# Values of a cross attention made for four pairs of heads at once, in 512 columns, and weights and x turned first

## The reference, cut to what matters

```
r = sigmoid(x @ Wr.T); k = x @ Wk.T; v = x @ Wv.T       # weights are made ternary first
state = cumsum(k*v / scale) * scale                      # over tokens
x = layernorm(x + rmsnorm(r*state, ln_w) @ Wo.T)
q = x @ Wq + bq; k = ctx @ Wk + bk; v = ctx @ Wv + bv    # 16 heads of 64
x = layernorm(x + softmax(q k.T / 8) v @ Wo + bo)
x = layernorm(x + moe(x))     # top 1 of 8 experts, capacity 512, 128 -> 512 -> 128
```

## Time and profile before

| | us |
|---|---|
| median of 3 runs | 2730.99 (2728.54 to 2731.56) |
| profiled execution | 2729.38 |
| its span, first to last instruction | 2727.6 |
| TensorE busy | 2659.0 |
| VectorE busy | 2122.0 |
| GpSimd busy | 2152.3 |
| ScalarE busy | 1723.4 |
| mean granted clock of TensorE | 0.989 of 2.4 GHz |

### The profile page before, as it was taken

One profiled execution on the slowest core, in us unless ns is written; L12 is line 12 of the kernel. 1 busy time (PEld: TensorE's weight loads), 2 busy tenths in 40 slices (PEclk: granted clock), 3 DMA queues, 4 the chain that ended last, 5 costly groups with the idle time before them and its releaser, 6 DMA issues.

```text
span 2727.6 us, 67860 instructions
## 1 busy us (share of the span) xinstructions
PE 2659.0 (97%) x26920; PEld 2280.4 (84%) x26920; DVE 2122.0 (78%) x4293; ACT 1723.4 (63%) x3470; POOL 2152.3 (79%) x1749
## 2 busy tenths in 40 slices
PE   5999999999999999999999999999999999999977
PEld 5888888888888888888888888888888888888855
DVE  6687878788787887878778787878878788787744
ACT  3666676666666666756657666666666666666632
POOL 1778888888788877888878888888888787888845
PEclk7999999999999999999999999999999999999988
DMA  4000000000000000000000000000000000000030
GB/s 101 7 22 7 27 10 9 24 8 27 9 8 25 11 23 10 21 12 11 26 7 22 11 25 11 8 24 9 25 9 23 10 10 23 8 11 9 12 99 27
DMA packets 81086, 53.28 MB, mean 20 GB/s; under 512 B 14239, under 2 KB 78453, under 8 KB 80768
## 3 DMA queue, kind: packets, MB, share of 16 engines
q1 hardware_dynamic: 75600, 45.27, 5.9%
q0 software_dynamic: 2048, 3.66, 0.4%
q10 hardware_dynamic: 3120, 0.01, 0.1%
HBM read 40.76 MB, written 8.72 MB: 18 GB/s over the span
## 4 chain that ended last, share of the span: by engine, by line
PE 95%; DVE 2%; POOL 1%; issue 1%; ACT 1%; DMA 0%; SPq 0%; POOLq 0%; DVEq 0%; ACTq 0%
PE ps L1484 26%; PE ps L1452 22%; PE ps L1448 10%; PE ps L1439 5%; PE ps L1430 4%; PE ps L1432 4%; PE ps L1431 4%; PE ps L1409 3%; PE ps L1411 3%; PE ps L1410 3%; PE ps L1500 3%; PE ps L1524 2%; PE ps L1385 1%; POOL out_dram L694 1%; PE ps L1367 1%
## 5 line engine op out<-in xcount | busy, mean ns | idle before, releaser
L622 POOL TENSOR_TENSOR key_sums<-key_sums,prob_T 65x512 f32<-65x512 f32 x1402 | 1816.2, 1295 | 161.7 <-POOL key_sums L622 2.2
L1048 DVE TENSOR_REDUCE mx<-ps 128x1 f32<-128x400 f32 (+1 forms) x2048 | 1055.9, 569 | 249.5 <-PE ps L1439 208.5
L818 ACT ACTIVATE prob_T<-ps 128x512 f32<-128x512 f32 x1536 | 832.8, 596 | 92.8 <-PE ps L1452 54.3
L1484 PE MATMUL ps<-prob_T,v_sb 128*64 128x256 f32 (+1 forms) x6656 | 740.5, 379 | 0.8 <-ACT prob_T L818 0.8
L1452 PE MATMUL ps<-q_hi,k_hi 64*128 64x256 f32 (+1 forms) x3328 | 734.8, 278 | 1.4 <-ACT prob_T L818 1.4
L1452 PE MATMUL ps<-q_lo,k_hi 64*128 64x256 f32 (+1 forms) x3328 | 732.8, 277 | 0.0
L1452 PE MATMUL ps<-q_hi,k_lo 64*128 64x256 f32 (+1 forms) x3328 | 731.6, 277 | 0.0
L1484 PEld LDWEIGHTS ps<-prob_T,v_sb 128*64 128x64 f32 (+1 forms) x6656 | 478.2, 137 | 241.4 <-ACT prob_T L818 1.7
L1452 PEld LDWEIGHTS ps<-q_hi,k_hi 64*128 64x128 f32 (+1 forms) x3328 | 578.0, 180 | 7.4 <-ACT prob_T L818 6.7
L1439 PE MATMUL ps<-k_hi,q_hi 64*128 64x400 f32 (+1 forms) x2048 | 580.4, 351 | 1.2 <-DVE q_lo L1039 1.2
L1448 PE MATMUL ps<-shift,shift_w 64*128 64x512 f32 (+1 forms) x1792 | 562.0, 381 | 2.7 <-ACT shift L789 1.4
(11 more groups left out here) (198 smaller groups left out, 3580.1 us busy)
## 6 DMA issues: line engine op xcount, KB each, us to landing
shift_f<-row_shifts SPq DMA_DIRECT2D x256, 64.0 KB, 2.6
ctx_raw<-in_ctx_dram SPq DMA_DIRECT2D x16, 768.0 KB
row_shifts<-nm_T SPq DMA_DIRECT2D x512, 0.5 KB
prob_T<-in_L_ffn_W_dram SPq DMA_DIRECT2D x12, 256.0 KB, 5.1
slots_in<-no_row SPq DMA_DIRECT2D x1, 2080.0 KB, 14.3
v_sb<-slots_in SPq DMA_DIRECT2D x8, 260.0 KB, 5.8
x_in<-in_x_dram SPq DMA_DIRECT2D x8, 256.0 KB, 2.9
out_dram<-x1s SPq DMA_DIRECT2D x16, 128.0 KB, 4.0
```

The costliest lines, as they stand in the source:

```text
L622: op = nc.gpsimd.tensor_tensor(acc[0:rows, :, :], acc[0:rows, :, :], prob_T[0:rows, :, k, :], ALU.add)
L818: nc.scalar.activation(prob_T[:, h, 2 * i - 2:2 * i, :].rearrange("p k t -> p (k t)"), ps[:, bank, :], ACT.Exp).then_inc(ring_act, 1)
L1048: v.tensor_reduce(mx[:, qt, h, c:c + 1], ps[:, at.bank("mx", r, c, qt, h), 0:WID[c]], AX.X, ALU.max).then_inc(ring_dve, 1)
L1484: last = mm(ps[h * DH:h * DH + DH, bank, 0:T], v_sb[0:rows, r % NJ // 2 % 2, k, v0 + h * DH:v0 + h * DH + DH], prob_T[0:rows, h, k, :], st ...
```

## The change

Values are made for four pairs at once. One fill is now one key tile of 512 columns, three matmuls, so a group has 13 fills; two groups a batch. They are made in the slots of the pairs 0 and 4 that use them first, about a quarter before each of the four key fills; group 0 of the first batch in the prologue. `v_sb` has one half of the same total size; its first copy waits for the product of the pair before, and `attend` also waits for the last fill's copy. In the prologue TensorE turns the weights and x first, then the context; ScalarE scales the fourth weight instead of VectorE; GpSimd makes the fourth weight ternary and writes the constants of the decay tables; the weights lie in `prob_T`'s region instead of `v_sb`'s; the low part of Wv is made ahead of the root mean square; values come ahead of x1; VectorE makes two low parts of keys ahead of the residual, and Wq's low part behind the norm.

```diff
-V_FILLS = 7
-V_FIRST = 4
+V_FILLS = 13
+V_PAIRS = 4
-def value_fills(s):
-    group = s // 2 + 1
-    return [("v", group, n) for n in (range(V_FIRST, V_FILLS) if s % 2 else range(V_FIRST))]
+def value_fills(r):
+    fills = [("v", r // V_PAIRS, n) for n in range(V_FILLS if r % V_PAIRS == 0 and r > 0 else 0)]
+    return [fills[len(fills) * i // 4:len(fills) * (i + 1) // 4] for i in range(4)]
...
-        v_sb = sb("v_sb", [P, 2, KT, 2 * P])
+        v_sb = sb("v_sb", [P, KT, V_PAIRS * P])
...
+            pool.wait_ge(tern_in, 16 * 6)
+            pool.wait_ge(thresholds, 1)
+            own(nc.gpsimd.tensor_scalar(w_tmp[:, 3, :], w_rows[:, 3, :], w_half[:, 3:4], None, ALU.is_gt))
...
+            nc.gpsimd.tensor_tensor(w_tern[:, 3, :], w_rows[:, 3, :], w_tmp[:, 3, :], ALU.subtract).then_inc(tern_out, 1)
...
-                    if at.kind != "first" or g > 1:
-                        act.wait_ge(ring_full, at.full("pv", 2 * g - 3))
+                    act.wait_ge(ring_full, at.full("pv", V_PAIRS * g - 1))
+                rows = P if n < KT - 1 else KREM
+                copy(v_sb[0:rows, n, :], ps[0:rows, at.bank("v", g, n), :]).then_inc(ring_act, 1)
...
+            nc.scalar.activation(w_T[:, 3, :], ps[:, 7, 3 * P:4 * P], ACT.Copy, scale=lnw_c[:, :]).then_inc(setup_ev_act, 1)
...
-            dve.wait_ge(setup_tr, 1)
-            dve.wait_ge(setup_ev_act, 1)
-            v.tensor_scalar(w_T[:, 3, :], ps[:, 7, 3 * P:4 * P], lnw_c[:, :], None, ALU.mult)\
-                .then_inc(setup_ev_dve, 1)
...
             def values(at, g, n):
-                bank, g0 = bank_of(at, "v", g, n), g % 4 * 2 * P
-                tiles = (2 * n, 2 * n + 1) if n < V_FILLS - 1 else (KT - 1,)
-                for i, k in enumerate(tiles):
...
+                bank = bank_of(at, "v", g, n)
+                rows = P if n < KT - 1 else KREM
+                o, cols = ps[0:rows, bank, :], slice(n * P, n * P + rows)
+                weights = slice(g % 2 * V_PAIRS * P, (g % 2 + 1) * V_PAIRS * P)
+                mm(o, ctx_hi[:, cols], wv_hi[:, weights], start=True, stop=False)
+                mm(o, ctx_hi[:, cols], wv_lo[:, weights], start=False, stop=False)
+                mm(o, ctx_lo[:, cols], wv_hi[:, weights], start=False, stop=True).then_inc(ring_full, 1)
...
-                bank, = banks_of(at, ("pv", r), also=[("s", r, UNITS - 1, 1)])
+                bank, = banks_of(at, ("pv", r), also=[("s", r, UNITS - 1, 1), ("v", r // V_PAIRS, V_FILLS - 1)])
...
             at = start
+            turn_weights()
+            step_tokens(at, 0)
             for c in range(4):
                 context(at, 0, c)
-            turn_weights()
-            step_tokens(at, 0)
...
             for c in range(4):
                 keys(at, 0, c)
+            pe.wait_ge(wv_split, 1)
+            for n in range(V_FILLS):
+                values(at, 0, n)
             step_x1(at, 0)
```

More of the change, by code:

```diff
@@ L80, in maximum @@
         put("dve", "mx", r, *unit, h)
+    step(0, "xt")
     for c in range(4):
         put("dve", "ctx", 0, c)
-    step(0, "xt", "r", "kk", "vv", "o", "ss")
+    step(0, "r", "kk", "vv", "o", "ss")
     for c in range(4):
         put("dve", "k", 0, c)
+    for n in range(V_FILLS):
+        put("act", "v", 0, n)
     step(0, "x1t")
@@ L113, in all_fills @@
                 step(step_of(b, batches), "x1t")
-            some = value_fills(s) if after else []
+            lots = value_fills(r)
             for i in range(4):
-                if i < len(some):
-                    put("act", "v", 4 * b + some[i][1], some[i][2])
+                for key in lots[i]:
+                    put("act", *key)
                 if after:
@@ L347, in decoder_layer @@
         heads_T = sb("heads_T", [P, NJ, T])
[L350 to L353, removed]
+        wq_rows, wk_rows, wv_rows = (region[:, n * AD:(n + 1) * AD] for n in range(3))
+        w_rows, w_tmp, w_tern = (region[:, 3 * AD + n * 4 * P:3 * AD + (n + 1) * 4 * P].rearrange(
+            "p (m n) -> p m n", n=P) for n in range(3))
+        assert 3 * AD + 12 * P <= 2 * KT * T
+        spare = v_sb[:, :, :].rearrange("p k n -> p (k n)")
         EW = F + FC * P
@@ L836, in batch @@
                         x1T_out(at, step)
-                    some = value_fills(s) if after else []
+                    lots = value_fills(at.b * NJ + s)
                     for i in range(4):
-                        if i < len(some):
-                            values_out(at, *some[i][1:])
+                        for _, group, n in lots[i]:
+                            values_out(at, group - 2 * at.b, n)
                         if after:
@@ L881, in _ @@
                 keys_high(at, 0, c)
+            for n in range(V_FILLS):
+                values_out(at, 0, n)
             x1T_out(at, 0)
@@ L1245, in _ @@
             gated(at, 0)
+            mean_square(at, 0)
+            dve.wait_ge(biases_in, 16 * 3)
+            v.tensor_scalar(bq_s[:, :], bq_c[:, :], SCALE, None, ALU.mult).then_inc(wq_split, 1)
+            for c in range(2):
+                keys_low(at, 0, c)
+            residual(at, 0)
+            step_moments(0)
+            for c in range(2, 4):
+                keys_low(at, 0, c)
+            normed(0)
             dve.wait_ge(wq_in, 16)
@@ L1569, in batch @@
                         context_read(at, 1)
-                    some = value_fills(s) if after else []
+                    lots = value_fills(at.b * NJ + s)
                     for i in range(4):
-                        if i < len(some):
-                            values(at, *some[i][1:])
+                        for _, group, n in lots[i]:
+                            values(at, group - 2 * at.b, n)
                         if after:
@@ L1618, in _ @@
                 maximum(at, 0, *unit, 0)
-            pe.wait_ge(wv_split, 1)
-            for n in range(V_FILLS):
-                values(at, 0, n)
             for c in range(4):
```

71 lines of the change are left out of this document (29 added, 42 removed).

## The result

| | before | after |
|---|---|---|
| median of 10 runs each, us | 2730.11 (2728.54 to 2731.56) | 2736.93 (2733.62 to 2739.07) |
| profiled execution, its span | 2729.4, 2727.6 | 2738.2, 2736.4 |
| first score of the loop | 62.07 | 62.20 |
| first score of the last slot | 2606.70 | 2614.06 |
| from there to the end | 120.88 | 122.33 |

The ratio is 1.0025, interval 1.0016 to 1.0035: 6.8 us slower by the medians, 8.8 by the profiled executions. The forecast was 2735, a change of 3.7 us, too small to be told from none (under 5.5 us), in a range that holds 2736.9. The time is right to 2 us; the difference lies just beyond those 5.5 us. The profiled 8.8 us fall 7.2 into the loop, 0.1 ahead of it and 1.5 behind it.

What follows compares the result with a forecast made beforehand. The prediction took TensorE's own stream, busy 97% of the span, as the bound, plus each wait the change adds. Its terms, -11.4 + 6.1 + 4.5 + 2.5 + 2 = +3.7 us, gave 2735 us, range 2716 to 2750.

Steps and rivals of the forecast that it cites:

- 512 columns, 63 old groups to 31 new: Value matmuls in the loop: 0.231 us per 512 columns against two of 0.1183, 290.7 to 279.3 us, -11.4 us.
- (a): Slot 2 of odd batches: the moments make VectorE late and TensorE stalls 0.87 us in the next scores, seven times, +6.1 us.
- (b): Slot 3 of even batches: the scan makes heads_T and ScalarE's exponentials late, TensorE stalls 0.65 us in seven batches, +4.5 us.
- destinations: Slot 6, where VectorE makes the destinations: said to come out 0.1 us inside the limit, put at 0.
- (c): Next pair's shift, through DRAM and back: margin 0.7 us in short slots, a few longer round trips, +2.5 us (0 to 15).
- (d): Slots 0 and 4: the product with the values waits for the 13th fill's copy, hidden by other work, nothing.
- first scores: End of the prologue: scores begin at 62.1 against 62.07 us, so no gain from the reordering, 0 us.
- clock of the first slot: After 5 us without work ahead of the first scores, TensorE runs at 1.2 GHz for a while, +2 us (0 to 4).
- The first rival: Value matmuls: 512 columns hide a cost of each matmul and take 0.2133 us; 2714 us, chance 0.1.
- The second rival: Short slots: VectorE's lateness doesn't reach TensorE, since banks lend more or locked operations move; (a) and (b) go, 2724 us, chance 0.18.
- The third: Rival: first scores behind slots 1, 2, 3, 5, 6, 7 wait for the shift chain, 13 us; 2748 us, chance 0.2.
- the fourth: Rival in the prologue: values ahead of x1 run at 1.2 GHz and delay the maxima by 7 us; 2742 us, chance 0.12.

Runs made afterwards that it cites:

- e1: Changed kernel with each value fill as six matmuls of 256 columns instead of three of 512: 2740.23 us, ratio 1.0038 to the kernel before.
- e3: Changed kernel with all 13 prologue value fills behind the first maxima instead of ahead of x1: 2735.55 us, ratio 1.0021 to the kernel before.
- e4: Changed kernel with the step's moments moved from slot 2 of odd batches to behind the residual in slot 0: 2731.60 us, ratio 1.0010.
- e5: Changed kernel with the step's scan moved from slot 3 to slot 4 of even batches: 2735.53 us, ratio 1.0021 to the kernel before.
- e7: Changed kernel with 3 prologue value fills ahead of x1 and 10 behind the first maxima: 2733.61 us, ratio 1.0012 to the kernel before.
- e6: Changed kernel with VectorE's last four operations of the destinations moved from slot 6 to slot 7: 2728.57 us, ratio 0.9998 to the kernel before.
- e2: Kernel before with the new prologue alone, its old loop and seven 256-column fills behind the maxima kept: 2726.05 us, ratio 0.9985.
- e10: e2 plus the three VectorE moves of e4, e5 and e6 in the old loop: 2741.55 us, ratio 1.0043 to the kernel before.
- e8: Changed kernel with the edits of e4, e5, e6 and e7 together: 2724.35 us, ratio 0.9978 to the kernel before.
- e9: e2 with 3 of its 7 prologue value fills ahead of x1 and 4 behind the maxima: 2724.76 us, ratio 0.9982 to the kernel before.

## Why the prediction came out as it did

| term, us | forecast | measured |
|---|---|---|
| 512 columns, 63 old groups to 31 new | -11.4 | -8.9 (1209 x 0.2331 = 281.8) |
| (a) moments | +6.1 | +2.2 (slots 3, five of seven odd batches) |
| (b) scan | +4.5 | +1.8 (slots 4, batches 4 to 12, over what was there) |
| destinations | 0 | +6.9 (slots 7 of batches 1 to 14) |
| (c) the shift | +2.5 | +1.1 (4 new waits) |
| (d) the 13th copy | 0 | 0 (no such wait in the trace) |
| first scores | 0 | +0.1 |
| clock of the first slot | +2 | +2.8 in this execution |
| behind the last slot | 0 | +1.5 in this execution |

The slot terms are sums over the slots, after less before, less what the fills there cost (0.1183 and 0.2331 us a matmul). The measured terms sum to 7.5, the spans differ by 8.8; of the other 1.3 us, 1.0 is in slot 6 of batches 2, 6, 10 and 14 (17.08 in place of 16.81), and its cause is open. The end took 120.9 to 122.4 us in six kernels with the same end (the changed one, e1, e3, e4, e5, e7), so the last term is scatter as well as anything.

**Luck.** That the sum of 3.7 came so near is in good part luck: (a) and (b) were 6.6 us too high and the destinations 6.9 too low, and these cancel. The first term was 2.5 too favourable, (c) 1.4 too high, and the end 1.5 too low.

**The step that failed** is the sentence "The slots with the destinations (slot 6) come out 0.1 us inside; I put 0." The rule of (a) applied to the border of pair 39 denies it: 0.75 us late before, + 2.84 by the fills, - 1.01 that VectorE gains = 2.58, against the limit of 1.89 - 0.57 = 1.32. The prediction shows no working for its 0.1 us inside. The same rule would have asked 1.26 us of each of 15 batches, 19 us, far too much; but it names the place. That slot ends with a chain of ten operations, and no row of it was read to the end. e6 shows the term by taking it away.

**(a) and (b)** had the right mechanism, place and limit. (a): 1.75 late less a stall of 0.48 is 1.27, pair 39's 1.82 less 0.57 is 1.25, the forecast's limit 1.32. What was mis-sized is VectorE's gain by coming to the keys earlier: 1.01 from two rows, 1.45 measured in slot 2 (0.36 late before, + 2.84 - 1.75), 1.43 in slot 3, 1.77 in slot 6. In slots 2 and 3 no later k_lo had waited; what is shorter is an operation between them, ve_a in slot 2 from 1.23 to 0.97 us, the scan in slot 3 from 2.22 to 1.92. In slot 6 two more waits of 0.62 us before k_lo went, and top gave 1.04 back (0.16 before, 1.20 after). Nor do (a) and (b) fall on seven batches each, but on five. In batches 7 and 9 the shift held up the first score of slot 3 by 0.42 and 0.33 us, VectorE was 1.25 and 1.33 late there instead of 1.75, and TensorE lost 0.0 and 0.1. e4 takes (a) away, and e5 all of (b) that the change had added.

**The first rival**, a cost of each matmul that 512 columns hide, is out: 0.2331 us, not 0.2133, and e1 adds only 4.5 us in its slots. The gap rule of the Trainium skill (TensorE: Matmul & The Clock Gate, "Wait — 56ns, not 53.3ns?"), 512/2.4 + 2.5 = 216 ns, doesn't hold for these float32r operands: 233 ns is measured, and the measurement decides. At 1.2 GHz the trace agrees with that section's N/1.2: 32.91 to 33.34, 0.43 us.

**The second rival** is out, though not by much: lateness does reach TensorE, from about 1.3 us on. 1.25 us late cost nothing, 1.60 to 1.62 (batches 2, 6, 10) 0.30 to 0.32, and 1.82 (batch 4) 0.51. Below that the banks lend it, which is why the slots before showed so little, with VectorE 0.36 and 0.75 late. **The third** didn't happen: of the 5 waits for the shift in the loop (7.0 - 4.56 = 2.4 us) four are new, 0.2 to 0.4 each; the fifth, 1.34 at the last slot, stood there before the change too (1.35). Nor did **the fourth**: the values ran at 2.4 GHz from 34.19 on.

**The prologue**: first products at 17.67 (17 expected) and keys at 28.76 (29.2) confirm the order of weights and context, and e2 its worth. Of the clock, had 0.50 from 41 to 46 before. Behind the new gap of 4.56 us the first slot had 0.84, with 2.8 us lost; in e4 and e5, with the same prologue but a wait of 2.57 and 2.33 us there, the clock stayed at 1.00 and the slot took 16.7. In e6, with a wait of 4.53 us, it had 0.92 and took 17.96. So this term isn't in every execution, which may be why the medians differ by 2 us less than the profiles. It fits that the two fastest of the changed kernel's ten runs, 2733.62 and 2734.73, are the two with the highest mean clock (0.991); it isn't shown, as only one of the ten has a trace.

## What to carry to other kernels

When slots are made shorter, make a table of every slot kind with what the second engine does last in it, and apply one limit (here 1.3 us behind the first score) to all of them: the one left out cost 6.9 us, the two worked out 4.0 together. Unequal slots want the side work in the long ones (e4, e5), and equal ones have no room for it (e10). Each moved operation is to be followed to the DMA and the queue that hang on it (e8). Fill both gaps of a prologue in part (e7, e9) rather than one of them whole.

## What was not expected of the hardware

- Two VectorE operations on 128x2 elements took 1.10 and 1.20 us beside GpSimd's additions, each of 1.28 us and about 1.38 from start to start. In the stretch behind the last slot, where GpSimd has no work (it is idle until 2644.97), the same lines took:

```profile
2643.33 0.17 DVE L1192 TENSOR_SCALAR keep<-rank 128x2 f32<-128x2 f32 x1
...
2643.72 0.16 DVE L1195 TENSOR_TENSOR top<-slot,keep 128x2 f32<-128x2 f32 x1
```

  The two additions beside them:

```profile
840.33 1.27 POOL L643 TENSOR_TENSOR key_sums<-key_sums,prob_T 128x512 f32<-128x512 f32 x1
...
841.75 1.28 POOL L643 TENSOR_TENSOR key_sums<-key_sums,prob_T 128x512 f32<-128x512 f32 x1
```

  The VectorE operations end at 841.62 and 843.06, the additions at 841.60 and 843.03. The operation between them, L1194, took 0.16 in both places: it starts at 841.66, between two additions. The Trainium skill (SBUF — State Buffer, on the shared port pair) has the loser blocked for the whole instruction; the trace agrees. So an operation of 0.16 us costs whatever is left of the addition beside it. In the kernel before, top took 0.16 us in 14 of the loop's 15 batches with destinations; now it takes 1.17 to 1.21 in all 15, so the change moved it beside an addition. By these durations VectorE would have been 2 us earlier at that border without the two, and nothing late; no run shows that.
- A matmul of these float32r operands costs nearly the same for each column at 2.4 GHz: 0.1183 us for 256, 0.1817 for 400, 0.2331 for 512, which is 0.462, 0.454 and 0.455 ns a column.
- The same prologue came out in two ways. In e4 and e5 the last key fill ahead of the scores still ran at 1.2 GHz (0.333 us a matmul of 400), TensorE then waited 2.57 and 2.33 us and kept 2.4 GHz; in the changed kernel that fill ran at 2.4 GHz already, the wait was 4.56 us, and the scores began at 1.2 GHz. Why the fill differed is open.
